# Layer 1's attention in four column tiles, normalization in three Vector operations

## The reference

```python
def _layernorm(x, axis=-1, eps=1e-05):
    m = jnp.mean(x, axis=axis, keepdims=True)
    v = jnp.var(x, axis=axis, keepdims=True)
    return (x - m) / jnp.sqrt(v + eps)
...
# layer 1's attention: 16 heads of 8, 64 features
qf = jax.nn.relu(q @ Wf + bf)
kf = jax.nn.relu(k @ Wf + bf)
kv = jnp.einsum('blhf,blhd->bhfd', kf, v)
out = jnp.einsum('blhf,bhfd->blhd', qf, kv)
k_sum = kf.sum(axis=1)
normalizer = jnp.einsum('blhf,bhf->blh', qf, k_sum)[..., None]
normalizer = jnp.maximum(normalizer, 1e-06)
out = (out / normalizer).reshape(b, l, d)
return out @ Wo + bo
```

## Time and profile before

| | before |
|---|---|
| median of 3 runs | 2178.87 us (2173.84 to 2181.28) |
| the profiled execution | 2177.14 us, of which the span from first to last instruction 2175.3 |
| TensorE (PE) busy | 1766.4 us, 81% |
| VectorE (DVE) busy | 1394.1 us, 64% |
| ScalarE (ACT) busy | 928.3 us, 43% |
| GpSimd (POOL) busy | 766.7 us, 35% |
| mean granted TensorE clock | 0.881 |

### The profile page before, as it was taken

How to read it: one execution, slowest core, us unless ns; L and a number is a source line. 1 busy time by engine, 2 the same in 40 slices (tenths; PEclk the granted TensorE clock), 3 DMA queues, 4 the chain that set the end, 5 groups by cost and what they waited for, 6 DMA issues and landing times.

```text
span 2175.3 us, 28709 instructions
## 1 busy us (share of the span) xinstructions
PE 1766.4 (81%) x10554; PEld 1006.2 (46%) x10554; DVE 1394.1 (64%) x3180; ACT 928.3 (43%) x1615; POOL 766.7 (35%) x662
## 2 busy tenths in 40 slices
PE   7888798667888888777698987886778898788677
PEld 3466565113445666423154765641234565564114
DVE  4663455998565344797955534569984554457996
ACT  3443233444444323445444533345444453335543
POOL 1220111786122010475712201138741230114892
PEclk9999999678999989988898998986878999889679
DMA  6003411121000341202000034023100003302210
GB/s 194 1 1 96 125 30 56 54 75 30 11 1 2 95 125 30 78 25 83 30 10 0 5 108 122 17 69 94 42 11 5 1 21 107 99 25 83 80 43 10
DMA packets 96589, 113.86 MB, mean 52 GB/s; under 512 B 7616, under 2 KB 70848, under 8 KB 96192
## 3 DMA queue, kind: packets, MB, share of 16 engines
q1 hardware_dynamic: 94400, 107.83, 16.7%
q0 software_dynamic: 2048, 4.20, 0.6%
HBM read 89.06 MB, written 22.94 MB: 51 GB/s over the span
## 4 chain that ended last, share of the span: by engine, by line
PE 50%; DVE 20%; POOL 8%; ACT 6%; issue 6%; DMA 6%; SPq 4%; DVEq 0%; POOLq 0%; ACTq 0%
PE P L223 8%; DVE M L1929 7%; POOL M L1999 5%; PE P L1552 4%; PE P L1772 3%; DMA W<-in_e 3%; PE P L1760 2%; PE P L1135 2%; PE P L894 2%; PE P L920 2%; SPq L1375 2%; PE P L1140 2%; DVE M L196 2%; PE P L345 2%; PE P L212 2%
## 5 line engine op out<-in xcount | busy, mean ns | idle before, releaser
L1929 DVE TENSOR_TENSOR_SCAN M<-P,M 128x512 f32<-128x512 f32 x384 | 444.7, 1203 | 22.9 <-POOL M L1999 12.2
L1760 PE MATMUL P<-M,wt 32*32 32x512 f32 x3072 | 281.9, 804 | 170.2 <-DVE M L1929 106.4
L1843 ACT ACTIVATE P<-M,negA 128x512 f32<-128x512 f32 x384 | 263.7, 690 | 258.8 <-DVE M L1929 242.0
L223 PEld LDWEIGHTS P<-wt,M 128*128 128x128 f32 x2176 | 277.6, 194 | 95.2 <-issue 35.9
L223 PE MATMUL P<-wt,M 128*128 128x128 f32 x2176 | 291.0, 280 | 13.2 <-ACT M L455 3.5
L1999 POOL TENSOR_TENSOR M<-M 128x512 f32<-128x512 f32 x192 | 245.1, 1309 | 159.0 <-DMA M<-du 123.7
L1999 POOL TENSOR_TENSOR M<-W,M 128x512 f32<-128x512 f32 x192 | 239.7, 1281 | 40.3 <-PE P L1760 40.1
L1760 PEld LDWEIGHTS P<-M,wt 32*32 32x32 f32 x3072 | 40.0, 118 | 371.6 <-DVE M L1929 260.7
L204 POOL TENSOR_TENSOR st<-st,wt 128x4 f32<-128x4 f32 x64 | 65.1, 1017 | 358.0 <-DVE st L192 354.6
L1552 PE MATMUL P<-M,wt 128*128 128x512 f32 x256 | 140.0, 630 | 7.3 <-ACT M L1601 7.2
L1649 DVE TENSOR_TENSOR M<-M,P 128x512 f32<-128x512 f32 x128 | 87.1, 682 | 87.7 <-PE P L1560 87.5
(11 more groups left out here) (331 smaller groups left out, 3338.6 us busy)
## 6 DMA issues: line engine op xcount, KB each, us to landing
W<-in_e SPq DMA_DIRECT2D x152, 192.0 KB, 2.5
M<-dt SPq DMA_DIRECT2D x64, 256.0 KB, 5.1
M<-xs SPq DMA_DIRECT2D x32, 256.0 KB, 4.4
ys<-M SPq DMA_DIRECT2D x32, 256.0 KB, 2.2
M<-du SPq DMA_DIRECT2D x32, 256.0 KB, 5.2
W<-du SPq DMA_DIRECT2D x32, 256.0 KB, 5.6
W<-xh SPq DMA_DIRECT2D x16, 256.0 KB
xs<-zero SPq DMA_DIRECT2D x2, 1216.0 KB, 9.8
```

The costliest lines, as they stand in the source:

```text
L223: m = e.matmul(out[:, tok(j)], h[:, tok(j)], wgt, start=first and j == 0, stop=last, skip_group_check=True)
L1760: m = e.matmul(t["sums"][i // 2][to:to + 32, :], part("WC", c)[r, r], scan[r, :], start=c == 0, stop=c == 5, tile_position=(32 * i, to))
L1843: e.activation(t["aa"][n % 2][:, :], t["dtr"][i][:, :], EXP, scale=negA[:, c:c + 1]).then_inc(ACT.s, ACT.mark(b, "a3", "aa", n))
L1929: e.tensor_tensor_scan(bb[:, :], t["aa"][n % 2][:, :], bb[:, :], 0.0, MUL, ADD).then_inc(DVE.s, DVE.mark(b, "a3", "scan", n))
```

## The change

**Normalization.** Vector subtracts the mean from the whole 128x512 in one tensor_tensor operation right behind L192, without waiting for GpSimd, and after GpSimd's result multiplies in two halves of 128x256. TensorE's transposes wait for a half instead of a quarter.

**Layer 1's attention.** The key-value product has 18 columns a pair. The products of the query features of four pairs are issued together, each with 32 output rows in its own column tile of the array (`tile_position=(0, 32 * k)`), and don't accumulate. There are eight buffers `qf`, so ScalarE waits for no product before it writes one. `kvm` is 32 columns a pair, of which 18 are written and 14 zeroed by GpSimd with one more memset a batch. The stacked operands and weights are used with all 128 rows (rows 98 to 127 of the weights are zero). The copies out and the transposes have 128 rows. The division and the rows of the output weights follow the new places of the heads.

**The order.** All five strings of `TURNS` are new; TensorE's has 48 turns less, six for each batch.

```diff
             e.tensor_scalar(st[:, 32:36], var, 1e-5, None, ADD).then_inc(DVE.s, DVE.mark(b, tag, "var"))
+            mean = st[:, 24:32].rearrange("p (j c) -> p j c", c=2)[:, :, 0]
+            e.tensor_tensor(v3(xk[:, :], 4), v3(x, 4), mean.unsqueeze(2).to_broadcast([128, 4, 128]), SUB).then_inc(
+                DVE.s, DVE.mark(b, tag, "xc"))
             yield
             w.wait_ge(POOL.s, POOL.of(b, tag, "rstd"))
-            for j in range(4):
-                e.tensor_scalar(xk[:, tok(j)], x[:, tok(j)], st[:, 24 + 2 * j:25 + 2 * j], st[:, 36 + j:37 + j],
-                                SUB, MUL).then_inc(DVE.s, DVE.mark(b, tag, "xk", j))
+            w.wait_ge(DVE.s, DVE.of(b, tag, "xc"))
+            for i in range(2):
+                half = xk[:, 256 * i:256 * i + 256].rearrange("p (j c) -> p j c", j=2)
+                e.tensor_tensor(half, half, st[:, 36 + 2 * i:38 + 2 * i].unsqueeze(2).to_broadcast([128, 2, 128]),
+                                MUL).then_inc(DVE.s, DVE.mark(b, tag, "xk", i))
...
-                w.wait_ge(DVE.s, DVE.of(b, tag, "xk", j))
+                w.wait_ge(DVE.s, DVE.of(b, tag, "xk", j // 2))
                 e.transpose(P[1][:, tok(j)], xk[:, tok(j)], ident).then_inc(PE.s, PE.mark(b, tag, "xT"))
...
-            xn, qf, kf = T_[0], T_[5:7], T_[7:9]
+            xn, qf, kf = T_[0], T_[22:26] + T_[18:21] + T_[9:10], T_[7:9]
...
-            kvm = L.M[:, 17 * T:17 * T + 576].rearrange("p (c n) -> p c n", c=8)
+            kvm = L.M[:, 17 * T:17 * T + 256].rearrange("p (c n) -> p c n", c=8)
...
-                                 kst[g % 2][0:98, 256 * i + 128 * j:256 * i + 128 * j + 128], wfs[0:98, :],
+                                 kst[g % 2][:, 256 * i + 128 * j:256 * i + 128 * j + 128], wfs[:, :],
                                  start=True, stop=True)
...
-                e.matmul(a1_bank(L, A1_QF[c])[:, :], wfs[0:98, 128 * (c % 2):128 * (c % 2) + 128], qst[g % 2][0:98, :],
+                e.matmul(a1_bank(L, A1_QF[c])[:, :], wfs[:, 128 * (c % 2):128 * (c % 2) + 128], qst[g % 2][:, :],
                          start=True, stop=True).then_inc(PE.s, PE.mark(b, "a1", "qf", c))
...
-                        m = e.matmul(P[2 + h][:, 72 * (c % 4):72 * (c % 4) + 72],
+                        m = e.matmul(P[2 + h][:, 18 * (c % 4):18 * (c % 4) + 18],
                                      kf[i][:, 256 * j + 128 * (c % 2):256 * j + 128 * (c % 2) + 128],
-                                     va[:, 2 * i + j, 8 * h:8 * h + 8, :].rearrange("p h c -> p (h c)"),
+                                     va[:, 2 * i + j, 2 * c:2 * c + 2, :].rearrange("p h c -> p (h c)"),
                                      start=i == 0 and j == 0 and c % 4 == 0, stop=i == 1 and j == 1,
                                      skip_group_check=True)
                 m.then_inc(PE.s, PE.mark(b, "a1", "kv", u))
...
-                g = c // 4
-                yield
-                w.wait_ge(ACT.s, ACT.of(b, "a1", "qf", c))
-                w.wait_ge(DVE.s, DVE.of(b, "a1", "kvm", g))
-                e.matmul(P[2 + g][0:72, :], kvm[:, c, :], qf[c % 2][:, :], start=c % 4 == 0, stop=c % 4 == 3).then_inc(
-                    PE.s, PE.mark(b, "a1", "qkv", c))
+                if c % 4 == 3:
+                    g = c // 4
+                    yield
+                    w.wait_ge(ACT.s, ACT.of(b, "a1", "qf", c))
+                    w.wait_ge(DVE.s, DVE.of(b, "a1", "kvm", g))
+                    for k in range(4):
+                        m = e.matmul(P[2 + g][32 * k:32 * k + 32, :], kvm[:, 4 * g + k, :], qf[4 * g + k][:, :],
+                                     start=True, stop=True, tile_position=(0, 32 * k))
+                    m.then_inc(PE.s, PE.mark(b, "a1", "qkv", g))
             for i, z in enumerate((oA, oB)):
                 yield
                 w.wait_ge(ACT.s, ACT.of(b, "a1", "o", i))
                 for j in range(4):
-                    m = e.transpose(P[i][:, 72 * j:72 * j + 72], z[0:72, tok(j)], ident[0:72, 0:72])
+                    m = e.transpose(P[i][:, tok(j)], z[:, tok(j)], ident)
                 m.then_inc(PE.s, PE.mark(b, "a1", "oT", i))
...
-                if c > 1:
-                    w.wait_ge(PE.s, PE.of(b, "a1", "qkv", c - 2))
-                e.activation(qf[c % 2][:, :], a1_bank(L, A1_QF[c])[:, :], RELU).then_inc(
+                e.activation(qf[c][:, :], a1_bank(L, A1_QF[c])[:, :], RELU).then_inc(
...
-                    w.wait_ge(PE.s, PE.of(b, "a1", "qkv", 3))
-                    e.activation(oA[0:72, :], P[2][0:72, :], COPY).then_inc(ACT.s, ACT.mark(b, "a1", "o", 0))
-            yield
-            w.wait_ge(PE.s, PE.of(b, "a1", "qkv", 7))
-            e.activation(oB[0:72, :], P[3][0:72, :], COPY).then_inc(ACT.s, ACT.mark(b, "a1", "o", 1))
+                    w.wait_ge(PE.s, PE.of(b, "a1", "qkv", 0))
+                    e.activation(oA[:, :], P[2][:, :], COPY).then_inc(ACT.s, ACT.mark(b, "a1", "o", 0))
+            yield
+            w.wait_ge(PE.s, PE.of(b, "a1", "qkv", 1))
+            e.activation(oB[:, :], P[3][:, :], COPY).then_inc(ACT.s, ACT.mark(b, "a1", "o", 1))
...
-                    e.tensor_tensor(kvm[:, 0:4, :], v3(P[2][:, 0:288], 4), v3(wv("kvmask"), 4), MUL).then_inc(
+                    e.tensor_tensor(kvm[:, 0:4, 0:18], v3(P[2][:, 0:72], 4), over_tokens(wv("kvmask")), MUL).then_inc(
                         DVE.s, DVE.mark(b, "a1", "kvm", 0))
...
-                src = P[i][:, 0:288].rearrange("p (w h c) -> p w h c", w=4, c=9)
-                rd = sm[:, 32 * i:32 * i + 32].rearrange("p (w h) -> p w h", w=4)
+                src = P[i][:, :].rearrange("p (a r) -> p a r", r=32)[:, :, 0:18].rearrange("p a (h c) -> p a h c", c=9)
+                rd = sm[:, 32 * i:32 * i + 32].rearrange("p (a h) -> p a h", h=2)
...
-                e.tensor_tensor(oq[:, :].rearrange("p (w g h c) -> p w g h c", w=4, g=2, c=8)[:, :, i], src[:, :, :, 0:8],
-                                rd.unsqueeze(3).to_broadcast([128, 4, 8, 8]), MUL).then_inc(
+                e.tensor_tensor(oq[:, :].rearrange("p (a g h c) -> p a g h c", a=16, g=2, c=8)[:, :, i], src[:, :, :, 0:8],
+                                rd.unsqueeze(3).to_broadcast([128, 16, 2, 8]), MUL).then_inc(
                     DVE.s, DVE.mark(b, "a1", "on"))
...
             e.memset(L.M[:, T:T + 576], 1.0)
+            e.memset(L.M[:, 17 * T:17 * T + 256], 0.0)
...
-            w.wait_ge(DVE.s, DVE.of(b, "a1", "xk", 3))
+            w.wait_ge(DVE.s, DVE.of(b, "a1", "xk", 1))
...
-            "tensor": (2243,
-                "00000021d041065b7fe14bfffda1e1041c9880000015701f36ffff1198c3fef6b3cfe1fee3c3c1e03a00000b4f056401e6bf"
...
+            "tensor": (2195,
+                "41e808241b2a0820cbd7f0b3bffc0fe100000424c20f5fe18d1fd05ec61f870ff71ff087a1c21d00e4000003ce107be1e4ef"
...
-    for n, k in (("a1q", "Wq"), ("a1k", "Wk"), ("a1v", "Wv"), ("a1o", "Wo")):
+    for n, k in (("a1q", "Wq"), ("a1k", "Wk"), ("a1v", "Wv")):
         add(n, np.asarray(I["L1_attn_" + k]))
+    add("a1o", np.asarray(I["L1_attn_Wo"]).reshape(2, 4, 2, 8, 128).transpose(1, 0, 2, 3, 4).reshape(128, 128))
     add("a1bo", rows(I["L1_attn_bo"]))
...
-    km = np.zeros((128, 4, 72), f)
-    for c in range(4):
-        km[0:64, c, 18 * c:18 * c + 9] = 1
-        km[64:128, c, 18 * c + 9:18 * c + 18] = 1
-    add("kvmask", km.reshape(128, -1))
+    km = np.zeros((128, 18), f)
+    km[0:64, 0:9] = km[64:128, 9:18] = 1
+    add("kvmask", km)
```

More of the change, by code:

```diff
@@ L1039, in dve_attn1 @@
             w.wait_ge(PE.s, PE.of(b, "a1", "kv", 7))
-            e.tensor_tensor(kvm[:, 4:8, :], v3(P[3][:, 0:288], 4), v3(wv("kvmask"), 4), MUL).then_inc(
+            e.tensor_tensor(kvm[:, 4:8, 0:18], v3(P[3][:, 0:72], 4), over_tokens(wv("kvmask")), MUL).then_inc(
                 DVE.s, DVE.mark(b, "a1", "kvm", 1))
@@ L2169, in program @@
+                "0000bb80ff7b5fc809760084af65f3a6ebf4a71f7039c3402fc1ba185ea9000550080aafc05feff6dffffffe027ff05bffff"
+                "ff1004f181a83fdfddbfe80b4184dc0771608fc63cbffa1822f7a156feb5ffef6ac0feb008000000000e3fe00163ffffff10"
+                "04f181a83fefddbfe80b4184dc0771c7e98e3c72ff0053de855777d2ffef5581fd7010000000000e3fe00"),
             "vector": (2343,
-                "00000001fff871502df800000000816cfdfbd7ffff03017e406000c203fff3ffebffe01b0280a05007eabbcfd4d549717d2c"
-                "05f5f42a4a00503d54000067fd556fafffae82dff2801f91efa9001fff0f40bf13bd0000000079fef5ffffff03017e404800"
@@ L2172, in program @@
-                "054ffdbff5fff3f8480180c0a006fabba000afa1ffc03e888000000064959769cf81ef000fffffffffffffc6007e47b79200"
-                "7ffcae057c4ef4000001e03fa7fdfef7ffff03000200108039ffcfffafff806c0a02814017d5e79fa892eae93e04facbe952"
-                "2a807a150000067faaaefaad05bffd55416e00000ffffe1ea7caf8bfff800000012a7f3fbf7bfffffc0c00010008203ffe7f"
-                "affffd0140601800c3037d5cf01fa457fc297a92a4cbe9522a807aa802ffffdef9cfffffe60d5501ffe07e"),
```

(12 more changed lines are left out.)

15 lines of the change are left out of this document (6 added, 9 removed).

## The result

The changed kernel takes 2234.44 us (median of 4 runs, 2233.04 to 2237.1); the kernel before, run beside it, 2176.36 (4 runs). The medians lie 58 us apart. The ratio on record, by which this document goes, is 1.0242, 95% interval 1.0212 to 1.0273: **slower by 2.4%**, where 1.8% faster was forecast.

What follows compares the result with a forecast made beforehand. PE was taken to bound the stretch holding most of the edit, at full clock. Terms -27 + 1 - 7 - 5 = -38 on 2175.3 us gave 2137.3, so 2139 us, 1.8% faster; forecast 2122 to 2158, with rivals 2100 to 2170.

Steps and rivals of the forecast that it cites:

- I give it nothing: Key-value product L894: 18 columns instead of 72 save 0, since the weight load sets the pace of either.
- I take -5 us: New turns at the seams between batch pairs: lanes finishing and starting together give -5 us, bounds -57 and +34.
- 548 us a pair: Seams: estimated length of a batch pair without overlap, 528 plus about 20 us of ffn0; two pairs 1096 against 1098 before.
- rival C: Attention 0 and ffn0: lanes in step lose each other's cover, PE under 85%, 2200 us; chance 0.09.
- C's second price: ffn0 of b4 to b7: power operation L769 without attention 1 beside it, 4 x 5.56 = 22 us idle PE.
- Column tiles, -27 us: Layer 1's attention, L920: PE gives back 37.6 us after longer transposes, worth -27 us; bounds -38 and -10.
- factor of 73%: L920: 41 of its 56 us of PE are on the chain, so 37.6 us saved count as 27.
- rival B: Attention 1's tail: the wait moves to ScalarE's eight 0.6-us activations, gain only 10 us, 2156 us; chance 0.08.
- Normalization, -7 us: Normalization L196: 11 us saved on the chain less 4 us of added DVE time; bounds -18 and +15.
- so it is hidden either way: Normalization: the 128x512 mean subtraction, 0.68 to 0.97 us, fits behind GpSimd's 1.02-us reciprocal root L204.
- Rival D: Normalization costs DVE time and saves none, +15 for -7, 2161 us, as the tensor_scalar rate rule implies; chance 0.05.
- Smaller edits, +1 us: GpSimd's extra 0.31-us memset before the power operation in eight batches, half on the chain: +1 us; rows and masks nothing.

Runs made afterwards that it cites:

- order alone: The kernel before with nothing changed but the table of turns, which is the changed kernel's on every engine: 1.0127 [1.0097, 1.0157].
- mixed order: New turns up to batch 2's third feed-forward part, then old: on the kernel before 0.9995, with tiles 0.9952, on the changed kernel with 72 columns 0.9948.
- tiles alone: The kernel before with column tiles, eight feature buffers, full rows and the memset; 72-column product, old normalization and old turns kept: 0.999 [0.9973, 1.0008].
- doubled groups: The kernel with only the column-tile edit, each group of four tiled products issued twice: 1.0031 [1.0013, 1.005] against 0.999 without doubling.

## Why the prediction was wrong

The four parts taken by themselves account for the whole: tiles -0.1%, normalization 0.0, narrow product +1.3, order +1.3, together +2.5% against +2.42 measured. Within the intervals they add, and no interplay is needed. The one sum that fits less well is that of the three edits in the old order: +1.3 by the single runs, +0.7 (0.3 to 1.1) when run together.

**Key-value product, "I give it nothing": the step that failed first.** It asked only what paces the product, and had that right (0.81 us from the first of eight to the next instruction, with 18 columns and with 72). What it left out is what the product does to the clock. Streaming 18 columns instead of 72 costs 29 us alone and 31 when it is undone in the changed kernel. Neither the bounds (0 to -31) nor a rival had a loss there. Shown are the three facts: fewer columns, lower clock in the same stretch, and added time that is busy time of TensorE. With 18, 36, 72 and 120 columns the time is 1.3, 0.2, 0 and 0.1% over before, of which only the 1.3 is clear of noise; how the chip comes to it isn't visible here.

The page TensorE: Matmul & The Clock Gate of the Trainium skill says, under What's actually happening, that the gate gives either 1.2 or 2.4 GHz. The trace agrees: the same group of tiles takes 1.00 us in one place and 1.87 in another. Under HAM oscillation the page of the Trainium skill has, as its example of a clock that falls again and again, a kernel whose TensorE waits for DMA. Here it fell in a stretch where TensorE was busy 24.68 of 25 us (1210 to 1235).

**The order, "I take -5 us": the second.** It is +28 us by itself, near the upper bound (+34), and the sign was wrong. The working compared seams by estimated lengths (548 us a pair; it comes to -2 us, and -5 was taken), and assumed that lanes in step fill each other's waits as well as before. From the first output of the second pair to the end of the kernel, two pairs, it had 1096 us; order alone takes 1121.9 (1086.31 to 2208.2), before 1100.5 (1074.76 to 2175.3), and another 11.6 us are lost ahead of that output. It is what rival C, chance 0.09, describes: its mark was TensorE under 85% in attention 0 and ffn0. The windows of that part in the third pair, of the changed kernel and of before:

```profile
1101.00:1209.00 108.00, 88.83 (x417) 48.51 (x417) 56.17 (x156) 46.34 (x82) 20.54 (x21) 0.88 0.03 10
```

```profile
1074.00:1179.00 105.00, 93.25 (x423) 48.59 (x422) 61.59 (x177) 46.88 (x83) 20.47 (x21) 0.92 0.03 11
```

That is 82.2 and 88.8%; order alone has 85.5% (76.91 of 90 us, 1086 to 1176), just above the mark. The whole, 2234 us, lies beyond C's 2200, which had no loss for the narrow product. But C's second price, 22 us for GpSimd's 5.56-us operation, is not what was paid. That operation is on the chain four times before (22.8 us) and five times in order alone (27.5). In the waits of TensorE (us, times, longest) the added idle time is spread, order alone first, then before:

```profile
PE P L212 <- DVE M L196: 48.0, 18, 9.8
PE P L1135 <- DMA W<-in_e: 42.1, 23, 4.4
PE P L1125 <- DMA M<-xs: 25.3, 5, 8.3
```

```profile
PE P L212 <- DVE M L196: 42.6, 22, 9.0
PE P L1135 <- DMA W<-in_e: 37.7, 22, 3.8
PE P L1125 <- DMA M<-xs: 17.1, 4, 5.6
```

These three give 18 of 30 us, yet they are not what the order costs: the kernel before in the mixed order has 42.7, 42.5 and 31.2 us of them, 116.4 against 115.4 in order alone, and loses nothing. Between these two kernels, whose code is the same, 13 of 32 us are busy time of TensorE (1769.3 against 1756.3, mean granted clock 0.874 against 0.882) and the rest is idle time in many small waits, none of which differs by more than 9 us. Which turn causes the loss is open. Shown is the place (behind batch 2's third feed-forward part) and, against the kernel before, the kind (30 of 33 us are idle time); the last seam's overlap is excluded as the main part.

**Column tiles, -27 us: right mechanism, wrong worth.** TensorE gave back 20 to 27 of the 37.6 us, so the saving was itself too large, and the time moved by +0.1 to -0.3%. The step that failed is the factor of 73%, taken from the line's share of the chain. Being on the chain told where TensorE was last, not that the next wait was 27 us away; that wait (rival B: ScalarE, with its features and, more than B had it, its copies of the stacked q) stood right behind: 17 us of it in tiles alone against 2.6 before. In the mixed order the tiles give 0.4% (0.9952 against 0.9995, the intervals just touching), so perhaps 9 us can be had when the order fits. The doubled groups say only that time of TensorE is worth something in this tail.

**Normalization, -7 us: 0 measured.** The 4.95-us groups did go, but two halves beside GpSimd's work still last up to 2.89 us (409.79 on the chain above), and the power operation takes 1.34 instead of 1.02, which is 64 x 0.32 = 20 us on GpSimd. An undisturbed one in the changed kernel:

```profile
1674.05 0.17 DVE L192 TENSOR_SCALAR st<-st 128x4 f32<-128x4 f32 x1
...
1675.71 0.76 DVE L201 TENSOR_TENSOR M<-M,st 128x256 f32<-128x256 f32 x2 [0.90 <-POOL st L209]
```

The halves last 0.76 us, as forecast, instead of the 1.11 of the four operations. But they begin 1.49 us after L192 ends (1674.22 to 1675.71), where those began after 1.12 (1725.67 to 1726.79). What the halves give, 0.35 us, the wait takes back, 0.37. The step "so it is hidden either way" was wrong: the subtraction hides behind GpSimd's operation and makes it longer. The bounds (-18 to +15) held. Rival D was wrong as well: nothing was lost, and the prediction's figures for the rates of the two operations (0.42 us for 256 elements, 0.435 for 128) do not bear out a faster tensor_scalar, since 512 elements take 0.76 us in two halves and 1.11 in four tensor_scalar operations.

**Smaller edits, +1 us**: within what these runs can tell.

## What to carry to other kernels

A saving in work on the busiest engine is only worth what the order of the others lets through: test the edits in the old order and the new order on the old code before both are shipped together; here that pair of runs gives +0.7 and +1.3% of the 2.4, and tiles with the wide product and half of the new order give -0.5% instead. Don't count a float32 product with fewer columns as free: here eight records of 72 columns and eight of 18 both took 0.81 us to the next instruction at full clock, so there was nothing to win, and the 18 lost the clock. And where two lanes share the engines, compare the idle time of the busiest engine by stretch, not the overlap at the seams.
